# Attention scores from two float32r parts in 24 rows, four score matmuls as one group on the four quarters of the array

## The reference, cut to what matters

```python
# first: attention with a position bias, 2 sequences of 1024
logits = einsum('bhld,bhmd->bhlm', q, k) / sqrt(8) + bias[h, l - m]
x = x + layernorm(softmax(logits) @ v)            # q, k, v from layernorm(x) @ w_in
# second: attention without bias on the same tokens, then a mixture of experts
y = y + (softmax(q @ k.T / sqrt(8)) @ v) @ w_proj  # y = layernorm(x)
y = y + one expert of 8 per token (128 -> 512 -> 128, gelu)
x = x + layernorm(y)
```

## Time and profile before

| | before |
|---|---|
| median of 3 runs | 986.7 us (985.31 to 987.14) |
| the profiled execution | 982.6 us, its span 980.9 us |
| PE busy | 830.7 us (85%) |
| DVE busy | 750.7 us (77%) |
| ACT busy | 648.3 us (66%) |
| POOL busy | 136.7 us (14%) |
| stage 0, pass b | about 73 to 480 us |
| stage 1, pass b | about 552 to 846 us |

### The profile page before, as it was taken

One profiled execution on the slowest core, in us unless ns is written; L12 is line 12 of the kernel. 1 busy time (PEld: TensorE's weight loads), 2 busy tenths in 40 slices (PEclk: granted clock), 3 DMA queues, 4 the chain that ended last, 5 costly groups with the idle time before them and its releaser, 6 DMA issues.

```text
span 980.9 us, 22683 instructions
## 1 busy us (share of the span) xinstructions
PE 830.7 (85%) x9011; PEld 315.4 (32%) x9011; DVE 750.7 (77%) x1211; ACT 648.3 (66%) x1272; POOL 136.7 (14%) x376
## 2 busy tenths in 40 slices
PE   2449999999999999999735799999999999974770
PEld 1203333333333333333312122222222222354760
DVE  6477777777777777774297899999999999266544
ACT  5406777677777777777434499999999999710222
POOL 8100000000000000000010011011010110003772
PEclk9758999999999999999967599999999999975995
DMA  2654434444444443330005365322222121010123
GB/s 62 173 157 104 120 95 109 105 106 107 107 98 110 107 106 93 87 86 16 16 1 152 81 149 134 105 69 70 65 66 70 58 69 42 24 44 19 50 49 94
DMA packets 55609, 82.79 MB, mean 84 GB/s; under 512 B 12336, under 2 KB 42480, under 8 KB 55504
## 3 DMA queue, kind: packets, MB, share of 16 engines
q1 hardware_dynamic: 53648, 76.57, 29.6%
q0 software_dynamic: 1472, 3.02, 1.3%
q10 hardware_dynamic: 384, 1.76, 0.6%
HBM read 62.31 MB, written 19.01 MB: 83 GB/s over the span
## 4 chain that ended last, share of the span: by engine, by line
PE 65%; ACT 9%; DVE 7%; POOL 4%; issue 4%; DMA 2%; SPq 1%; DVEq 0%; POOLq 0%
PE bank L1155 22%; PE bank L1200 17%; PE bank L1207 14%; PE bank L1147 8%; ACT prob_mem L737 8%; POOL moe_out L653 2%; POOL prob_mem L642 2%; DVE stats L796 1%; DVE norm L810 1%; DVE unit_max L879 1%; PE bank L1362 1%; DMA prob_mem<-tokens,gather_u 1%; DVE meanvar L799 1%; PE bank L1372 1%; DMA k_parts<-prob_mem 0%
## 5 line engine op out<-in xcount | busy, mean ns | idle before, releaser
L737 ACT ACTIVATE prob_mem<-bank 128x512 f32<-128x512 f32 x1024 | 556.1, 597 | 137.8 <-PE bank L1207 120.3
L876 DVE CUSTOM_DVE_ANT_0 y_res<-bank,tables 128x1024 bf16<-128x1024 f32 x256 | 312.3, 1224 | 99.5 <-PE bank L1147 94.3
L1155 PE MATMUL bank<-prob_mem,v_ring 128*32 128x256 f32 x4096 | 320.2, 387 | 4.6 <-issue 2.6
L879 DVE TENSOR_REDUCE unit_max<-bank 128x1 f32<-128x1024 f32 x256 | 293.2, 1216 | 13.8 <-PE bank L1147 10.7
L1147 PE MATMUL bank<-k_rows,q_rows 56*128 56x512 bf16 x512 | 161.2, 418 | 44.6 <-DMA k_rows<-k_parts 30.2
L1200 PE MATMUL bank<-q_rows,k_rows 59*128 59x512 bf16 x512 | 164.2, 391 | 2.3 <-ACT prob_mem L737 0.7
L1200 PE MATMUL bank<-more_rows 59*128 59x512 bf16 x512 | 158.9, 383 | 3.1 <-ACT prob_mem L737 1.1
L1147 PE MATMUL bank<-more_rows 56*128 56x512 bf16 x512 | 159.0, 382 | 0.0
L1207 PE MATMUL bank<-feat,flip 96*32 96x512 bf16 x2048 | 158.8, 387 | 0.0
L1155 PEld LDWEIGHTS bank<-prob_mem,v_ring 128*32 128x32 f32 x4096 | 102.2, 109 | 159.8 <-ACT prob_mem L737 72.9
L598 POOL CAST max_parts<-unit_max 128x8 bf16<-128x8 f32 x64 | 12.1, 189 | 689.7 <-DVE unit_max L876 386.1
(11 more groups left out here) (160 smaller groups left out, 571.5 us busy)
## 6 DMA issues: line engine op xcount, KB each, us to landing
tables<-bias_rows SPq DMA_DIRECT2D x30, 480.0 KB, 5.3
unit_sums<-o_ring SPq DMA_DIRECT2D x64, 128.0 KB, 1.7
more_rows<-q_parts SPq DMA_DIRECT2D x64, 96.0 KB
more_rows<-k_parts SPq DMA_DIRECT2D x32, 192.0 KB
q_rows<-q_parts SPq DMA_DIRECT2D x56, 96.0 KB
k_rows<-k_parts SPq DMA_DIRECT2D x28, 192.0 KB
feat<-bias_parts SPq DMA_DIRECT2D x14, 378.0 KB, 3.8
w_moe<-in_L_ffn_w_dram SPq DMA_DIRECT2D x16, 256.0 KB, 3.8
```

The lines of the kernel that those rows point to most:

```text
L737: nc.scalar.activation(prob[:, kb, half * N:(half + 1) * N], b_bank(entry(ul, kb, half)), ACT.Exp).then_inc(exp_done[a], 1)
L876: nc.vector.tensor_tensor_reduce(out=no_use[qb % 2], in0=scores, in1=bias, scale=1.0, scalar=LEAST, op0=ALU.add, op1=ALU.max, accum_out=un ...
L879: nc.vector.tensor_reduce(unit_max[:, slot, qb:qb + 1], scores, AX.X, ALU.max).then_inc(max_done[1], 1)
L1155: ins = nc.tensor.matmul(AV[VM * c:VM * (c + 1), :], v_ring[:, head_slot, b * QB + kb, :], prob[:, kb, c * W:(c + 1) * W], start=(kb == 0) ...
```

## The change

q and k are kept as two parts in float32r (four bytes; the view `parts_r` of the same memory). ACT writes the first part, DVE the second; the middle step and `rest` go. A head's rows are 3 products times 8, `KR = 24`, with two more rows for the maxima (split in two). One tile `ring` holds four heads, 3072 columns each. Its four quarters of 32 partitions (`RG`) are pass a half 0, pass a half 1, pass b half 0, pass b half 1. In each quarter the first 2048 columns are the stationary operand and the last 1024 the moving half. `QK_DMAS` is 18. PE issues both waits for the banks and the wait for the slot first, and then the four score matmuls one after the other. POOL's four memsets become one. The tables of biases move into the memory of the expert weights, and two small tiles of the routing into `prob_mem`.

```diff
-    KR = 7 * DH
-    QK_DMAS = 10
+    KR = 3 * DH
+    RG = P // 4
+    QK_DMAS = 16 + 2
...
+        ring = sb("ring", [P, 4, T + T // 2])
+        ring_r = ring[:].bitcast(fp32r)
...
-            for rows in (32, 96):
-                chain(nc.gpsimd.memset(k_rows[rows:rows + 32], -1.0))
-                chain(nc.gpsimd.memset(more_rows[rows:rows + 32, 1], -1.0))
+            chain(nc.gpsimd.memset(ring[2 * RG:4 * RG, :, 0:T], -1.0))
...
-                    sp.dma_start(qp_dram[a][:, :, :, cols].rearrange("h d t n -> (h d) t n"),
-                                 parts[:, 0, :, cols]).then_inc(parts_stored[a], 16)
-                    sp.wait_ge(part_lo[a], 2 * g + 2)
-                    for t in range(3):
-                        sp.dma_start(kp_dram[a][:, t, :, cols], parts[:, 1, t, cols]).then_inc(parts_stored[a], 16)
+                    for s in range(2):
+                        sp.wait_ge(part_lo[a], 2 * g + s + 1)
+                        sp.dma_start((qp_dram, kp_dram)[s][a][:, :, :, cols].rearrange("h d t n -> (h d) t n"),
+                                     parts[:, s, :, cols]).then_inc(parts_stored[a], 16)
...
+                    head = (qp_dram, kp_dram)[s][a][bass.ds(h, 1)]
                     for f in range(2):
+                        for whole in (True, False):
+                            at = (2 * (s if whole else 1 - s) + f) * RG
+                            if whole:
+                                cols, off, inner = slice(b0 * L, b1 * L), b0 * L, [[1, (b1 - b0) * L]]
+                            else:
+                                cols, off, inner = slice(T + b0 * N, T + b1 * N), b0 * L + f * N, [[L, b1 - b0], [1, N]]
+                            twice = [[2 * T, DH], [0, 2]] if s == 0 else [[T, 2 * DH]]
+                            last = T if s == 0 else 0
+                            if whole or s:
+                                sp.dma_start(ring[at:at + 2 * DH, slot, cols],
+                                             bass.AP(head.tensor, head.offset + off, twice + inner)).then_inc(loaded, 16)
+                            else:
+                                for b in range(b0, b1):
+                                    sp.dma_start(ring[at:at + 2 * DH, slot, T + b * N:T + (b + 1) * N],
+                                                 bass.AP(head.tensor, head.offset + b * L + f * N, twice + [[1, N]])).then_inc(loaded, 16)
+                            sp.dma_start(ring[at + 2 * DH:at + KR, slot, cols],
+                                         bass.AP(head.tensor, head.offset + last + off, [[2 * T, DH]] + inner)).then_inc(loaded, 16)
...
-                    nc.scalar.copy(parts[:, 1, 0, cols], bank[:, 5 + 2 * (g % 2), :]).then_inc(part_hi[a], 1)
+                    nc.scalar.copy(parts_r[:, 1, 0, cols], bank[:, 5 + 2 * (g % 2), :]).then_inc(part_hi[a], 1)
...
-                    for s in range(2):
-                        act.wait_ge(part_rest[a], 2 * g + s + 1)
-                        nc.scalar.copy(parts[:, s, 1, cols], rest[:, g % 2, s, :]).then_inc(part_mid[a], 1)
...
-                        nc.vector.scalar_tensor_tensor(rest[:, g % 2, s, :], bank[:, 4 + 2 * (g % 2) + s, :], SCALE if s == 0 else 1.0,
-                                                       parts[:, s, 0, cols], ALU.mult, ALU.subtract).then_inc(part_rest[a], 1)
-                    for s in range(2):
-                        dve.wait_ge(part_mid[a], 2 * g + s + 1)
-                        nc.vector.tensor_tensor(parts[:, s, 2, cols], rest[:, g % 2, s, :], parts[:, s, 1, cols],
-                                                ALU.subtract).then_inc(part_lo[a], 1)
+                        nc.vector.scalar_tensor_tensor(parts_r[:, s, 1, cols], bank[:, 4 + 2 * (g % 2) + s, :], SCALE if s == 0 else 1.0,
+                                                       parts[:, s, 0, cols], ALU.mult, ALU.subtract).then_inc(part_lo[a], 1)
...
-                rows = slice(f * HP, f * HP + KR)
-                return nc.tensor.matmul(SA[slot][:, f, :], q_ring[head_slot][rows, b * L + qb * P:b * L + (qb + 1) * P],
-                                        k_ring[head_slot][rows, b * L + f * N:b * L + (f + 1) * N], start=True, stop=True)
+                rows = slice(f * RG, f * RG + KR)
+                return nc.tensor.matmul(SA[slot][:, f, :], ring_r[rows, head_slot, b * L + qb * P:b * L + (qb + 1) * P],
+                                        ring_r[rows, head_slot, T + b * N:T + (b + 1) * N], start=True, stop=True)
...
                             for f in range(2):
                                 b_bank_free(a, i, entry(ul, kb, f), first, last)
+                            if not done:
+                                pe.wait_ge(max_done[a], QB * (u + AU) + kb - 1)
+                            for f in range(2):
                                 ins = scores_b(a, ul, kb, f)
                                 if a == 1:
                                     ins.then_inc(sb_done[1], 1)
                                 if not done:
-                                    ins = block_a(a, u + AU, lu, kb, f == 0, (1 - f,))
+                                    ins = scores_a(kb % 2, (lu // B) % 4, lu % B, kb, f)
```

More of the change, by code:

```diff
@@ L8, in sandwich_kernel @@
                     ln2_w, ln2_b, gate_w, gate_b, w1, w2, out):
-    fp32, bf16 = mybir.dt.float32, mybir.dt.bfloat16
+    fp32, fp32r, bf16 = mybir.dt.float32, mybir.dt.float32r, mybir.dt.bfloat16
     ALU, ACT, AX = mybir.AluOpType, mybir.ActivationFunctionType, mybir.AxisListType
@@ L59, in sandwich_kernel @@
     moe_dram = nc.dram_tensor("moe_out", (T + NS * P, D), fp32, kind="Internal").ap()
[L61 to L62 removed]
+    qp_dram = [nc.dram_tensor(f"q_parts{a}", (H, DH, 2, T), fp32, kind="Internal").ap() for a in range(2)]
+    kp_dram = [nc.dram_tensor(f"k_parts{a}", (H, DH, 2, T), fp32, kind="Internal").ap() for a in range(2)]
     o_dram = nc.dram_tensor("unit_sums", (U, P, L // 4), fp32, kind="Internal").ap()
[L64 removed]
+    maxima_dram = nc.dram_tensor("maxima_rows", (2, 2 * QB, P), fp32, kind="Internal").ap()
     bias_dram = nc.dram_tensor("bias_rows", (H, 2 * L), fp32, kind="Internal").ap()
@@ L102, in sandwich_kernel @@
         bias_parts = prob_mem[:, 7168:7168 + 3 * N // 2].bitcast(bf16).rearrange("p (t n) -> p t n", t=3)
-        parts = prob_mem[:, 8192:14336].bitcast(bf16).rearrange("p (s t n) -> p s t n", s=2, t=3)
-        rest = prob_mem[:, 14336:16384].rearrange("p (r s n) -> p r s n", r=2, s=2)
+        parts = prob_mem[:, 8192:16384].rearrange("p (s t n) -> p s t n", s=2, t=2)
+        parts_r = prob_mem[:, 8192:16384].bitcast(fp32r).rearrange("p (s t n) -> p s t n", s=2, t=2)
         WE = 2 * HID
@@ L148, in sandwich_kernel @@
         unit_max = sb("unit_max", [P, 2, QB])
-        max_rest = sb("max_rest", [P, 2, QB])
-        max_parts = sb("max_parts", [P, 2, 3 * QB], bf16)
-        max_rows = sb("max_rows", [3 * QB, 2, P], bf16)
+        max_parts = sb("max_parts", [P, 2, 2 * QB])
+        max_parts_r = max_parts[:].bitcast(fp32r)
+        max_rows = sb("max_rows", [2 * QB, 2, P])
         gate = sb("gate", [P, TT, E])
@@ L226, in sandwich_kernel @@
         part_hi = [sem(f"part{a}_hi") for a in range(2)]
-        part_rest = [sem(f"part{a}_rest") for a in range(2)]
-        part_mid = [sem(f"part{a}_mid") for a in range(2)]
         part_lo = [sem(f"part{a}_lo") for a in range(2)]
@@ L325, in max_t @@
         def max_t(n):
-            return b_bank(n)[0:3 * QB, 0:P // 2].bitcast(bf16)
+            return b_bank(n)[0:2 * QB, 0:P]
         def table_of(queue, h, slot, half):
@@ L384, in store_parts, with rows_of @@
                             sp.dma_start(bp_dram[:, :, c * N:(c + 1) * N], bias_parts[VM * c:VM * c + H]).then_inc(bias_parts_stored, 16)
-                sp.wait_ge(parts_stored[a], 16 * 4 * (groups[-1] + 1))
-            def rows_of(a, h, slot, loaded, which=(0, 1), lo=0, hi=T):
+                sp.wait_ge(parts_stored[a], 16 * 2 * (groups[-1] + 1))
+            def rows_of(a, h, slot, loaded, which=(0, 1), b0=0, b1=B):
                 for s in which:
-                    ring = (q_ring, k_ring)[s][slot]
-                    one = (qp_dram, kp_dram)[s][a][bass.ds(h, 1), 0, 0, lo:hi]
-                    last = (qp_dram[a][bass.ds(h, 1), :, 0, lo:hi], kp_dram[a][bass.ds(h, 1), 2, :, lo:hi])[s]
+                    head = (qp_dram, kp_dram)[s][a][bass.ds(h, 1)]
@@ L392, in rows_of @@
                     for f in range(2):
-                        if s == 0:
-                            for r in range(2):
-                                sp.dma_start(ring[f * HP + 3 * DH * r:f * HP + 3 * DH * (r + 1), lo:hi],
-                                             bass.AP(one.tensor, one.offset, [[T, 3 * DH], [1, hi - lo]])).then_inc(loaded, 16)
-                        else:
-                            sp.dma_start(ring[f * HP:f * HP + 6 * DH, lo:hi],
```

(5 more changed lines are left out.)

70 lines of the change are left out of this document (28 added, 42 removed).

## The result

The changed kernel takes 1157.8 us (median of 1134.35, 1146.78, 1168.82 and 1170.03), the kernel before 986.9. The ratio of 1.156 [1.145, 1.167] sets the faster two of these runs against the kernel before, since the other two lie over 1.5% above the fastest. The forecast was 992.4 us with a range of 962 to 1030: the sign was right, the size was not. The runs lie further apart than those of before, and the mean granted clock goes with the time: 0.811, 0.805, 0.768 and 0.766 in the order above.

A forecast was written before the change was run, and what follows sets the result against it. PE was taken to set stage 0's pace, with DVE and the exponential ring close; in stage 1 DVE, ACT and PE were all over 96%. Terms -6.7 + 10.9 + 5 + 1 - 4.5 = +5.7 on 986.7 gave 992.4 us, range 962 to 1030.

The forecast's parts named there:

- One pass: Score matmuls: fp32r streams 512 columns in a single pass of 0.213 us, where full fp32 takes four.
- (c): Rival, score matmuls: fp32r takes two passes, s = 0.59, 1093 us in all; chance 0.07.
- (d): Rival, score matmuls: fp32r runs as fp32 in four passes, s = 1.02, about 1300 us; chance 0.02.
- s: Time of the four-matmul score group up to the bias matmuls: 0.38 us, including +0.05 for four-byte weight loads.
- (b): Rival, score group: four matmuls share the array less well, s = 0.52 (1028 us) or 0.44 (1009 us); chance 0.20.
- The ring of stage 0: PE-exponential loop per block: s + 1.10 us, block 3 s + 1.59; unit 12.33 us, -6.7 us over 32 units.
- The waits as part of the change: Bank and maxima waits moved ahead of the whole score group; counted within -6.7 us (stage 0) and +10.9 us (stage 1).
- Stage 1 at full clock: Stage 1 units: 1.12 us for six of eight steps, 9.60 us a unit, 0.34 more; +10.9 us over 32 units.
- The first units: Start of stage 1, where SP also issues expert weights and a unit's DMAs come near its length: +1 us.
- (e): Rival, stage 1: PE's clock falls; no time given, chance 0.03.
- Heads: Head of each stage: more loads in SP's queue at 0.43 us each, ahead of the maxima's store; +2.5 us a stage.
- Memset: Constants at the start: one POOL memset for four, ending before DVE's normalisations start; -4.5 us, bounds 0 and -5.8.

The follow-up runs named there:

- e5: The changed kernel with its parts, ring and maxima in bf16 instead of float32r (less exact scores): 1028.4 us.
- e2: The kernel before with all three waits moved ahead of the four score matmuls, rows and type unchanged: 1059.9 us.
- e3: The changed kernel with one extra 128-row, 512-column bf16 matmul (result unused) in each block of stage 1: 1107.0 us.
- e1: The kernel before with stage 1's score matmuls contracting 24 of their 56 and 59 rows, row maxima not subtracted: 1190.5 us.
- e11: The kernel before with 56 rows in both passes of stage 1, row maxima not subtracted: 985.8 us.
- e10: The changed kernel with one extra 24-row, 512-column bf16 matmul (result unused) in each block of stage 1: 1250.4 us.
- e13: The changed kernel with bf16 parts, ring and maxima, plus an extra 24-row bf16 matmul in each block of stage 1: 1194.3 us.
- e9: The kernel before with its four memsets written as four-byte values, half the elements, same bits: 973.0 us against 980.6, ratio 0.9931.

## Why the prediction was wrong, step by step

- **One pass**: right. Rivals (c) and (d) fell.
- **s, the group**: 0.38 predicted, 0.43 to 0.44 measured. Rival (b) is right in size (0.44 by the rule it cites), wrong in reason: four bf16 quarters take 0.32, as one pair of halves. The term mis-sized is the four-byte load: +0.11, not +0.05. Here a load is 0.18 us (303.07) against 0.09 in e5, and four of them aren't hidden.
- **The ring of stage 0**: s + 1.10 predicted, s + 1.15 measured (0.70 and not 0.65 from ACT to PE); block 3 s + 1.64, not s + 1.59; and block 0 of a unit 0.16 later, which wasn't in the sum. A unit: 8 x 0.05 + 7 x 0.05 + 0.05 + 0.16 = 0.96 more than 12.33, 13.29, and 13.32 was measured. The structure held, and the sign didn't: +24 us for 31 units where -6.5 stood. Another 9 us are late units near the start (16.17, 15.03 and 15.88 for 13.3): PE waits 2.56 us up to 121.68 for the maxima's load. Their store was issued at 116.11, behind a head's loads, and the load itself at 120.04, with nothing issued in between. The rest of these 9 us lies where the clock is 0.50 in stage 0 (124 to 130 and 192 to 198 us).
- **The waits as part of the change**: I weighed them only with s. e2 gives their price by itself: 1.6 us a unit of stage 0, 50 us there and 20 in stage 1, for a kernel whose scores take 0.54. A shorter group lowers it and doesn't remove it.
- **Stage 1 at full clock**: 9.60 a unit predicted, 10.28 measured (1.20 for an ordinary block against 1.12): s and the release again. The sum also took 1.12 for a block in which DVE alone needs 1.133, 0.08 us a unit too little. The first units were priced at +1 us in all; in after the low clock hides them, but e3, at clock 1.00 for most of stage 1, has 14.91, 17.06 and 11.56 for 11.0, 10.5 us more, some of it at clock 0.50.
- **(e), the clock**: the step that failed. It had a chance of 0.03 and no time, and it is some 100 of the 187 us between the two profiled spans. The runs show in its place: with 24 and 26 rows a matmul, in float32r, the granted clock is 0.50 for most of stage 1. The rows do it (e1 against e11, e10 against e3), together with the length of the block (e5 against e13). The evidence against it was read from the earlier trace rows at 840 to 845: a single pair and the values at clock 1.00. That pair has 59 rows in each half, 118 rows of the array. The row says nothing on 24. The time was at hand: the 0.64 us of streaming that I put in a block of 1.12 would double, which gives 1.76; 1.74 was measured. That it comes so close is luck in part: the 1.12 holds waits, and at the lower clock the block is PE's own 0.73 + 1.01.
- **Heads**: +2.5 a stage predicted; 5.0 and 12.8 measured, the first with the memset's gain of some 6 in it. Loads were priced at 0.43, the mean of before; the new shapes are up to 0.69, and the 34 loads from 53.62 us on take 18.1 us, 0.53 each. What makes the head of stage 1 dearer than that of stage 0 no run takes apart.
- **Memset**: right in its mechanism. One of 6.93 us, the twelve normalisations 3.24 us; -4.5 predicted, -6.4 at the first copy by e9 and -7.6 in its time, past the bound of -5.8. The 1.34 us each isn't in its row, which gives 8.93 / 12 = 0.74.

## What to carry to other kernels

Before packing thin matmuls on quarters of the array, ask what will keep TensorE's clock up: a stretch at clock 1.00 is evidence only for the rows of the array that work in it, and the price of half the clock belongs in the range as a number. Wait for the bank directly ahead of the matmul that needs it, and let the first pair go. Price a DMA's issue by its shape, and count the issues ahead of the first transfer that everything waits for.

## What the runs showed of the hardware

- In these runs TensorE's granted clock follows how much of the array works, not whether PE is busy: 24 rows for 56 brought 1190.5 for 985.8 us, at clock 0.50 for 1.00, with nothing else changed (e1, e11). One more matmul a block made a kernel faster with 128 rows (1158 to 1107) and slower with 24 (1250).
- float32r streams in one pass: one record of 0.47 to 0.50 us for 512 columns, where fp32 leaves two and takes 1.02. Its weight load lasts 0.18 us against 0.09 for bf16, and 0.28 at the lower clock; four of them at once cost 0.11 us, where four of bf16 cost nothing that can be seen.
- A group behind several waits starts 0.70 us after ACT's start of the instruction that releases it, in bf16 and in float32r (0.74 with the waits in another order), a single pair 0.65.
- POOL's memset takes its time by elements, not bytes: 1.80 us for 2048 of four bytes, 3.54 for 4096 of two.
